# The gated products written back into PSUM, and the low half of every third one made by GpSimd instead of VectorE

## The reference, cut to what matters

```python
g = jnp.einsum('bsd,edf->ebsf', h, Wg)          # 8 experts, D = 128, F = 512
u = jnp.einsum('bsd,edf->ebsf', h, Wu)
expert_outs = jnp.einsum('ebsf,efd->ebsd', jax.nn.silu(g) * u, Wd)
expert_output = jnp.einsum('be,ebsd->bsd', gating_probs, expert_outs)
shared = jnp.einsum('bsf,fd->bsd', jax.nn.silu(h @ Sg) * (h @ Su), Sd)
x = x + (1.0 - sg) * expert_output + sg * shared
```

## Time and profile before

| | |
|---|---|
| time, median of 3 runs | 530.17 us (528.30 to 530.59) |
| profiled execution, first to last instruction (span) | 526.8 us |
| PE busy | 467.7 us, 89% of the span |
| DVE busy | 367.4 us, 70% |
| ACT busy | 278.2 us, 53% |
| POOL busy | 195.5 us, 37% |
| round 0 / 1 / 2 / 3 (first gate products) | 16.5 to 152.0 / to 232 (233.82) / to about 316 (315.56) / to about 398 |

### The profile page before, as it was taken

The page is one execution under the profiler, slowest core; times in us unless marked ns, Lnnn a source line. Parts: engine busy times, 40 slices in busy tenths (PEclk is TensorE's granted clock), DMA queues, the critical chain, the costliest instruction groups (busy, mean ns, idle before and its releaser), DMA issues.

```text
span 526.8 us, 7084 instructions
## 1 busy us (share of the span) xinstructions
PE 467.7 (89%) x1894; PEld 340.5 (65%) x1894; DVE 367.4 (70%) x682; ACT 278.2 (53%) x592; POOL 195.5 (37%) x187
## 2 busy tenths in 40 slices
PE   5785887859699999999999999999997876999995
PEld 2674665648577877777877777788884533555542
DVE  6786695857466767667766667766875773888853
ACT  2654362726355555554655555656554453666663
POOL 4669294755322213141413232145772121222220
PEclk9989788989889999999999999999999997999998
DMA  5424133241200120000020000032216346555600
GB/s 163 111 70 142 57 107 115 73 128 41 75 9 0 29 74 2 0 1 0 10 92 0 0 0 0 1 102 62 62 29 190 83 121 179 163 165 164 168 22 21
DMA packets 44921, 37.29 MB, mean 71 GB/s; under 512 B 4408, under 2 KB 39388, under 8 KB 44892
## 3 DMA queue, kind: packets, MB, share of 16 engines
q1 hardware_dynamic: 43440, 36.64, 24.1%
q0 software_dynamic: 1024, 0.26, 0.3%
q10 hardware_dynamic: 432, 0.10, 0.1%
HBM read 26.07 MB, written 10.66 MB: 70 GB/s over the span
## 4 chain that ended last, share of the span: by engine, by line
PE 63%; DVE 12%; issue 8%; DMA 6%; SPq 4%; ACT 4%; POOL 1%; DVEq 0%; ACTq 0%; POOLq 0%
PE pv_ps L695 9%; PE acc_ps L521 6%; DVE act_lo L1057 5%; PE g_ps L521 5%; PE g_ps L523 5%; PE g_ps L522 5%; PE acc_ps L522 5%; PE acc_ps L523 5%; PE u_ps L521 4%; PE u_ps L522 4%; PE u_ps L523 4%; DMA v_d<-stage 3%; PE st_ps L684 2%; SPq L430 2%; DVE act_p L1053 2%
## 5 line engine op out<-in xcount | busy, mean ns | idle before, releaser
L802 ACT ACTIVATE act_p<-g_ps 128x512 f32<-128x512 f32 x144 | 86.2, 599 | 164.7 <-PE g_ps L523 161.0
L1053 DVE TENSOR_TENSOR act_p<-act_p,u_ps 128x512 f32<-128x512 f32 x144 | 98.7, 685 | 79.1 <-PE u_ps L523 75.0
L1057 DVE TENSOR_TENSOR act_lo<-act_p,act_hi 128x512 fp32r<-128x512 f32 x144 | 122.6, 851 | 0.2 <-ACT act_hi L807 0.2
L1257 POOL TENSOR_TENSOR xg_lo<-xg,xg_hi 128x512 fp32r<-128x512 f32 x35 | 50.7, 1450 | 165.9 <-ACT xg_hi L812 165.9
L807 ACT ACTIVATE act_hi<-act_p 128x512 fp32r<-128x512 f32 x144 | 89.8, 624 | 1.6 <-DVE act_p L1053 1.5
L695 PE MATMUL pv_ps<-probs_t,v_blocks 128*128 128x512 f32 x128 | 67.3, 608 | 3.1 <-ACT v_blocks L895 1.2
L521 PE MATMUL acc_ps<-act_hi,w_split 128*128 128x512 f32 x144 | 61.8, 429 | 7.8 <-DVE act_lo L1057 7.4
L887 ACT ACTIVATE probs_t<-st_ps 128x512 f32<-128x512 f32 x64 | 38.0, 595 | 43.0 <-PE st_ps L684 42.6
L521 PE MATMUL g_ps<-x_hi,w_split 128*128 128x512 f32 (+1 forms) x144 | 58.9, 409 | 1.4 <-DVE x_lo L1082 1.4
L521 PE MATMUL u_ps<-xg_hi,w_split 128*128 128x512 f32 x144 | 57.5, 400 | 0.1
L522 PE MATMUL g_ps<-x_lo,w_split 128*128 128x512 f32 (+1 forms) x144 | 57.5, 400 | 0.0
(11 more groups left out here) (147 smaller groups left out, 752.5 us busy)
## 6 DMA issues: line engine op xcount, KB each, us to landing
k_blocks<-k_rows SPq DMA_DIRECT2D x32, 96.0 KB
q_plain<-q_rows SPq DMA_DIRECT2D x8, 384.0 KB
q_blocks<-q_rows SPq DMA_DIRECT2D x32, 96.0 KB
k_plain<-k_rows SPq DMA_DIRECT2D x8, 384.0 KB
v_both<-v_d SPq DMA_DIRECT2D x8, 272.0 KB, 3.0
w_raw<-in_L_cond_Wg SPq DMA_DIRECT2D x8, 256.0 KB, 3.0
w_raw<-in_L_cond_Wu SPq DMA_DIRECT2D x8, 256.0 KB, 2.6
w_raw<-in_L_cond_Wd SPq DMA_DIRECT2D x8, 256.0 KB, 3.0
```

The source lines that it names most:

```text
L802: activation(act_p[k % 3][:], g_ps[k % 3][:], ACT.Silu).then_inc(silu_done, 1)
L1053: tt(act_p[k % 3][:], act_p[k % 3][:], u_ps[k % 3][:], ALU.mult).then_inc(prod_done, 1)
L1057: tt(act_lo[k % 3][:], act_p[k % 3][:], act_hi[k % 3][:].bitcast(F32), ALU.subtract).then_inc(act_lo_done, 1)
L1257: tt(xg_lo[e % 3][:], xg[:].rearrange("p b s -> p (b s)"), xg_hi[e % 3][:].bitcast(F32), ALU.subtract)\
```

## The change

Two things are changed together. In the slots with k % 3 of 0 or 1 the product goes back into the bank `u_ps[k % 3]` it came from, and ACT's rounding and DVE's subtraction read it there. In the slots with k % 3 == 2 the product still goes to `act_p` in SBUF, and the subtraction is made by POOL. The semaphore `act_lo_done` becomes two, one for each engine, and the waits that keep a buffer from being overwritten change with it: the up product of a slot whose bank holds a product waits for its `act_lo`, the silu of such a slot only for the product.

POOL's program is written out for all rounds, by slot instead of by expert: in each slot first the subtraction of chunk k - 1 if it is POOL's, then `gate_x` of the next expert if k % 4 == 1, `split_xg` if k % 4 == 2, then in round 3 the memsets, now in slot `FC * min(experts + 2, NE - 1) + 3`: 19, 27, 31 and 35.

```diff
+LO_TURN = 3
...
+        def by_pool(k):
+
+            return k % LO_TURN == LO_TURN - 1
...
+        def wait_low(eng, t, k):
+            if k < 0:
+                t, k = t - 1, k + SLOTS
...
+            turns = SLOTS // LO_TURN
+            if by_pool(k):
+                eng.wait_ge(act_lo_pool, t * turns + k // LO_TURN + 1)
+            else:
+                eng.wait_ge(act_lo_dve, t * (SLOTS - turns) + k - k // LO_TURN + 1)
...
-                wait(pe, prod_done, t * SLOTS + k - 2)
+                if by_pool(k):
+                    wait(pe, prod_done, t * SLOTS + k - 2)
+                else:
+                    wait_low(pe, t, k - 3)
...
-                pe.wait_ge(act_lo_done, t * SLOTS + k + 1)
+                wait_low(pe, t, k)
...
             def silu(t, k):
-                wait(act, act_lo_done, t * SLOTS + k - 2)
+                if by_pool(k):
+                    wait_low(act, t, k - 3)
+                else:
+                    wait(act, prod_done, t * SLOTS + k - 2)
...
-                activation(act_hi[k % 3][:], act_p[k % 3][:], ACT.Identity).then_inc(act_hi_done, 1)
+                activation(act_hi[k % 3][:], (act_p if by_pool(k) else u_ps)[k % 3][:], ACT.Identity).then_inc(act_hi_done, 1)
...
-                tt(act_p[k % 3][:], act_p[k % 3][:], u_ps[k % 3][:], ALU.mult).then_inc(prod_done, 1)
+                tt((act_p if by_pool(k) else u_ps)[k % 3][:], act_p[k % 3][:], u_ps[k % 3][:], ALU.mult).then_inc(prod_done, 1)
...
 @@ vector @@
             def split_act(t, k):
+                if by_pool(k):
+                    return
                 dve.wait_ge(act_hi_done, t * SLOTS + k + 1)
-                tt(act_lo[k % 3][:], act_p[k % 3][:], act_hi[k % 3][:].bitcast(F32), ALU.subtract).then_inc(act_lo_done, 1)
+                tt(act_lo[k % 3][:], u_ps[k % 3][:], act_hi[k % 3][:].bitcast(F32), ALU.subtract).then_inc(act_lo_dve, 1)
...
@@ gpsimd @@
+            def split_act(t, k):
+                if k < 0:
+                    t, k = t - 1, k + SLOTS
+                if t < 0 or not by_pool(k):
+                    return
+                pool.wait_ge(act_hi_done, t * SLOTS + k + 1)
+                tt(act_lo[k % 3][:], act_p[k % 3][:], act_hi[k % 3][:].bitcast(F32), ALU.subtract).then_inc(act_lo_pool, 1)
...
-            with pool.Fori(1, NT - 1) as t:
-                for e in range(NE):
-                    gate_x(t, e)
-                    split_xg(t, e)
-
-            for e in range(NE):
-                gate_x(NT - 1, e)
-                split_xg(NT - 1, e)
-                for tile, constant, experts in FILLS:
-                    if e == min(experts + 2, NE - 1):
...
+            for t in range(1, NT):
+                for k in range(SLOTS):
+                    e, c = divmod(k, FC)
+                    split_act(t, k - 1)
+                    if c == 1 and (t, e + 1) != (NT - 1, NE):
+                        gate_x(*((t, e + 1) if e + 1 < NE else (t + 1, 0)))
+                    if c == 2 and (t, e + 1) != (NT - 1, NE):
+                        split_xg(*((t, e + 1) if e + 1 < NE else (t + 1, 0)))
+                    for tile, constant, experts in FILLS:
+                        if t == NT - 1 and k == FC * min(experts + 2, NE - 1) + 3:
+                            pool.wait_ge(down_done, SLOTS * (NT - 1) + experts * FC)
+                            nc.gpsimd.memset(tile[:].bitcast(F32), constant).then_inc(blocks_filled, 1)
+            split_act(NT - 1, SLOTS - 1)
```

More of the change, by code:

```diff
@@ L252, in build @@
         silu_done, prod_done = sem("silu_done"), sem("prod_done")
-        act_hi_done, act_lo_done = sem("act_hi_done"), sem("act_lo_done")
+        act_hi_done = sem("act_hi_done")
+        act_lo_dve, act_lo_pool = sem("act_lo_dve"), sem("act_lo_pool")
         down_done = sem("down_done")
@@ L329, in placed @@
             return (b - n) * 16 + 32 * (n // 2 + 1)
+        def by_pool(k):
[3 more added lines that the diff above has]
+                t, k = t - 1, k + SLOTS
+            if isinstance(t, int) and t < 0:
+                return
[4 more added lines that the diff above has]
+                eng.wait_ge(act_lo_dve, t * (SLOTS - turns) + k - k // LO_TURN + 1)
         def wait(eng, semaphore, value):
@@ L1276, in _ @@
                 e, c = divmod(k, FC)
[L1277 to L1280, removed]
+                split_act(0, k - 1)
+                if c == 1:
+                    gate_x(*((0, e + 1) if e + 1 < NE else (1, 0)))
+                if c == 2:
+                    split_xg(*((0, e + 1) if e + 1 < NE else (1, 0)))
                 if e + 1 < NE and c < 3:
@@ L1289, in _ @@
                             make_mix(f, part)
-            with pool.Fori(1, NT - 1) as t:
-                for e in range(NE):
-                    gate_x(t, e)
-                    split_xg(t, e)
-            for e in range(NE):
-                gate_x(NT - 1, e)
-                split_xg(NT - 1, e)
-                for tile, constant, experts in FILLS:
-                    if e == min(experts + 2, NE - 1):
-                        pool.wait_ge(down_done, SLOTS * (NT - 1) + experts * FC)
-                        nc.gpsimd.memset(tile[:].bitcast(F32), constant).then_inc(blocks_filled, 1)
+            for t in range(1, NT):
[11 more added lines that the diff above has]
+            split_act(NT - 1, SLOTS - 1)
             def place_max(b, n):
```

## The result

The changed kernel takes **540.97 us** (median of 4 runs, 539.71 to 541.65) against 530.21 us (528.30 to 530.59) for the kernel before on the same chip: ratio **1.0217**, 95% interval 1.0181 to 1.0254. It is slower, as predicted, by 10.8 us; whether by more than 2% the interval leaves open. 545.3 us was forecast. The profiled execution has a span of 539.2 us against 526.8, which is 12.4 us more, and a mean granted clock of 0.935 against 0.958. The two differences are not the same: a profiled execution takes some 1.8 us more than its span, which makes the changed one 541.1 us, like its median, and the one before about 528.6, under its median of 530.2.

A forecast was written before the change was run, and what follows sets the result against it. PE was taken to bound rounds 1 to 3. Terms -7.1 + 6.7 + 6.9 + 2.0 + 5.8 + 0.8 = +15.1 us on the 526.8 span gave 541.9; with the median 3.4 above, 545.3 us, range 536 to 552.

The forecast's parts named there:

- Collisions, -7.1 us: Rounds 1 to 3: 14 slots lengthened by DVE's two-SBUF-input subtractions and POOL holding each other up would go, -7.1 us.
- DVE is still held: Rival: POOL still holds DVE's subtraction from PSUM, so the -7.1 us fall away: 552 us, chance 0.05.
- POOL's turn, +0.3 us each, +6.7: Rounds 1 to 3: POOL's 1.42 us subtraction makes PE's down product late, 0.3 us per affected chunk, +6.7 us.
- 23 waits: Sign: PE would wait for POOL's `act_lo` some 20 to 30 times, about 0.3 us each.
- First load, +6.9 us: Round 3: the first pair of memsets ends later, so PE's first early score waits for its load, +6.9 us.
- Clock behind it, +2.0: Round 3, behind the first score's wait: PE's clock falls to near half, +2.0 us, bounds 0 and 2.7.
- Loads of the attention, +5.8 us: Start of attention: late memsets delay SP's loads, `v_both` and PE's weighted sum, +5.8 us, bounds 2.7 and 8.
- Round 0, +0.8: Round 0: a POOL subtraction before `xg_lo` shifts SP's stores of projected rows, +0.8 us, bounds -2 and 4.
- no DVE subtraction above 0.75 us: Sign: in the profile after, no subtraction on DVE exceeds 0.75 us, with a mean near 0.69.
- 48 operations on POOL: Sign: the profile after shows 48 subtractions made by POOL, of about 1.43 us.
- the wait of 5.68 us for `q_plain`: Sign: before the first score PE waits above 4 us for the DMA of `q_plain` or `k_blocks`.
- POOL's mean of 1.43: Sign: POOL's 48 subtractions take about 1.43 us each in the profile after.

The follow-up runs named there:

- e4: Kernel before with only the product's write-back into PSUM, in every slot; DVE makes all low halves, POOL as before: 521.1 us, ratio 0.9794.
- e7: Changed kernel without the write-back, every product kept in SBUF; POOL's subtractions and the memsets' new places stay: 544.28 us, ratio 1.0269.
- e11: Changed kernel with none of POOL's subtractions; DVE makes all low halves from PSUM, POOL's new order stays: 532.64 us, ratio 1.0045.
- e12: Changed kernel with all POOL subtractions kept and each memset of the last round back behind its old `xg_lo`: 529.36 us, ratio 1.002.
- e3: Kernel before with only the first pair of memsets placed one expert later: 538.29 us, ratio 1.0131.
- e9: Changed kernel with POOL's subtractions of chunks 17, 32 and 35 given back to DVE, product in PSUM there too: 539.77 us, ratio 1.0195.
- e5: Changed kernel plus 24 matmuls whose results are never read, before the first score in slot 22 of round 3: 536.35 us, ratio 1.0109.
- e8: Kernel before with the write-back in every slot, plus 10 unread matmuls before the attention's first weighted sum: 517.59 us, ratio 0.9737.
- e1: Changed kernel with only the first pair of memsets moved from slot 19 back to slot 15 of round 3: 530.63 us, ratio 0.999.
- e2: Changed kernel with all eight memsets earlier, in slots 15, 15, 24, 24, 27, 27, 30 and 33: 531.62 us, ratio 1.0011.
- e10: Changed kernel with POOL making only the subtractions of chunks 17, 32 and 35, DVE the others from PSUM: 532.59 us, ratio 1.0062.

## Why the prediction was right, step by step

Direction and mechanism were right. The sum of +15.1 us was reckoned for the span, which grew by 12.4; the medians differ by 10.8. Of the 4.3 us between 545.3 and 540.97, 2.7 are the terms. The other 1.6 come from setting the median 3.4 us above the span: an execution takes some 1.8 us more than its span (541.1 against 539.2 in the changed kernel), and the rest was only that the profiled execution of the kernel before was a quick one. Two terms were off by 4.1 and 3.2 us in opposite directions; that the sum came as near as it did is in part luck.

- **Collisions, -7.1 us: confirmed** by e4 (-7.47). All 14 long slots are gone. The reason was incomplete: e7 shows that the rewritten order and POOL's turns take them off PE's path without the write-back. In the changed kernel the write-back is worth 0.4 us in rounds 1 to 3 and 2.2 in slots 24 to 34. The rival "DVE is still held" is excluded by the longest of its 96 subtractions, 0.69 us.
- **POOL's turn, +0.3 us each, +6.7: mis-sized.** It is 0.13 us a slot. Rounds 1 to 3 give -4.83 with turns and -7.46 without (e11): **2.6 us** (3.2 between e12 and e11). The failed step is the length of POOL's operation, taken as 1.42 us from a row in which DVE's subtractions with two SBUF inputs still ran; the change removes that very neighbour, and the operation is then 1.28. Put into the prediction's own chain, 1.28 gives 0.15 a slot. I used a duration that the change itself would alter, although the trace before already held the other one, in round 0:
```profile
24.47 1.29 POOL L1257 TENSOR_TENSOR xg_lo<-xg,xg_hi 128x512 fp32r<-128x512 f32 x1
```
  The count held: 23 waits against 20 to 30 foretold. (The text says five chunks for round 3 and lists six; the sum uses the six.)
- **First load, +6.9 us: met.** Slot 22 went from 2.28 to 9.15 us. e3 and e11 show that it is the place of the memsets behind the next `xg_lo`; e9 shows that the subtraction of chunk 17, which I had counted in the chain, is worth some 0.6 (9.15 against 8.58). I had the right end time of the chain with one link that hardly counts, since `xg_lo` waits for ACT anyway.
- **Clock behind it, +2.0: 1.2 us** (slot 23, 3.51 against 2.30). The clock was at 0.50 while PE worked from 370 to about 373. e5, with a full clock there, gives 1.6 for both slots.
- **Loads of the attention, +5.8 us: the tail lost 9.0.** `v_both` and the first weighted sum were 4.8 us late (for `v_both` 3.06 by the order, e11, and 1.77 by the subtractions in front of the late memsets). The missing term is the clock: behind the first weighted sum it was still at 0.50 and cost **3.4 us** up to the seventh (8.52 against 5.09). The last 0.8 us come later; there the second low stretch is 10 us long (0.53, 0.50 and 0.69 from 448 to 460) against 7 in the kernel before, which goes with it but isn't shown to be its cause. I had reckoned a slower clock behind the wait in slot 22 and not here, though PE waits here too, 1.71 us for the last `act_lo` of POOL and 2.00 us before the scores behind it.
- **Round 0, +0.8: -0.13**, within its bounds. No experiment singles it out; it varies more than this between kernels with the same work. (POOL's `w_split` vary from 1.26 to 2.13 us there, not to 1.78.)

Of the signs foretold, these came: no DVE subtraction above 0.75 us, 48 operations on POOL, 23 waits, the wait of 5.68 us for `q_plain`, `v_both` late, though by 4.83 and not 5.8. POOL's mean of 1.43 did not: it is 1.285.

## What to carry to other kernels

Find out first whether a duration in the trace includes a wait for a neighbour that your change removes; the same instruction elsewhere in the program, or one small experiment, tells. When a loop is rewritten to interleave new work, list what moved beside it: here eight memsets one expert later cost far more than the 48 operations that were the point of the change. The useful half of this edit alone, e4, is 2.1% faster, and e8 2.6%; test the halves of an edit one by one before judging it.

## What was not expected of the hardware

- POOL's operation is slowed by DVE, not only DVE's by POOL: 1450 ns beside subtractions with two SBUF inputs, 1303 once DVE reads PSUM (e4), 1351 when a third of them leave DVE (e7).
- DVE writes a product of 128 x 512 into PSUM in 694 to 695 ns against 686 to SBUF, and subtracts with one PSUM input in 683 ns, with two SBUF inputs and unheld in 685 (the 108 such of the kernel before). The Trainium skill, page "VectorE: DVE Perf Modes", section "The TRN2 errata", would make the PSUM source 65 ns dearer by its 62 cycles; the traces have no such surcharge.
- Behind PE's waits at the start of the attention the granted clock fell to 0.50 in some kernels and not in others: for some 7 us in e1, e2, e4, e5 and e10, 10 in e7, e9 and e11, 17 in the changed kernel, and not at all in e12 and the kernel before, whose longest waits there are 1.72 and 1.21 us (e4: 2.23). Ten unread matmuls kept it at 1.00 in e8. The low clock cost time only where PE had work again before it ended.
